# Window attention on the quarters of TensorE's array

## The chip, the cores and the metric

The kernel runs on one core of a Trainium2 chip. The metric is the device time of one execution in microseconds (us); lower is better. TensorE, VectorE (DVE), ScalarE (ACT), GpSimd (POOL) and the SP queue run their own instruction streams and meet through semaphores.

## The reference

Two layers in fp32 on x of shape (32, 56, 56, 48). Layer 0 makes a convolution per image from pooled features and adds it to x. Layer 1 is a shifted-window transformer block followed by a convolutional feed-forward part. The change lies in the attention part of layer 1, cut to what matters:

```python
h = roll(layer_norm(x) * g + b, (-3, -3))
xw = window_partition(h, 7)                 # 64 windows of 49 pixels per image
q, k, v = split_heads(xw @ w_qkv + b_qkv)   # 6 heads of 8
attn = softmax(q @ k.T * SCALE + rel_bias + mask)
o = (attn @ v) @ w_proj + b_proj
x = x + roll(window_reverse(o), (3, 3))
y = layer_norm(x)                           # goes to two convolutions with a GELU between
```

## The kernel before

Three stages run one after the other: `layer0`, `attention`, `feed_forward`. Layer 0 leaves its result in HBM as row chunks (`x1s`), attention writes x (`x2s`) and the second normalized y (`ys`), and the last stage reads both. Only `attention` is changed, with the constants and the packed weights that it uses.

Attention works on 128 chunks. A chunk is one row of 8 windows (7 pixel rows of 56) of two images; image 0 has its 48 channels on partitions 0 to 47, image 1 on 64 to 111. `each_chunk` calls `body` for the first two and last two chunks and in two loops of two chunks per turn between them. Each engine has its own `body`, an order written out by hand, in which work of four chunks is mixed: `body(n)` computes scores and softmax of chunk n, the normalization, queries, keys and value rows of n + 1, the output and projection of n - 1, and the second normalization of n - 2.

What one chunk does, before the change:

- `center` (L716): a matmul subtracts the channel mean. ScalarE copies the result (`xc`) and squares it twice, as fp32 and as a rounded part `sq_hi`; GpSimd makes `sq_lo`. `variance` sums both with two fp32r matmuls (L719, L720). ScalarE takes the logarithm and the exponential (L847, L851), VectorE multiplies to `h` (L1036), GpSimd copies `h` twice (L600).
- `queries`, `keys` (L716): one matmul each over both images. ScalarE writes the queries into a block-diagonal `qbd` in two parts (L859), GpSimd expands the keys to one masked copy per head, `kex`, one instruction per window (L614).
- `scores` (L674): per window one matmul with 98 weight columns (49 queries of two images) and 294 moving columns (49 keys of 6 heads). VectorE adds bias and mask per window (L1013), takes the maximum per duo of windows (L1025) and subtracts it (L1029); in the second duo GpSimd subtracts (L604). ScalarE takes the exponential (L882).
- `transposes` (L685): six per duo into the one buffer `ps_t`; ScalarE copies them to `pt` (L889), and the next duo's transposes wait for that copy (`pt_set`).
- `value_rows` (L745): per window one matmul; VectorE masks and copies (L1071). `values` (L700): per half chunk (4 windows) 24 matmuls for two heads at once, alternately on the left and right column half of the array. VectorE takes the reciprocal of the denominators and multiplies (L1045, L1049).
- `outputs` (L711) brings the result back to channels, ScalarE copies it (L874), `project` (L716) applies the projection, and VectorE adds the residual in two parts (L1061, L1063), rolled back by 3 pixels.
- `center2`, `variance2`, ScalarE and GpSimd: the second normalization, with the same split squares (L591); ScalarE applies the affine (L912).

An fp32 matmul is issued as two passes, each a weight load and a matmul; the trace counts passes. A transpose is one pass. SP issues eight DMAs per chunk: two loads of `xin`, two of `xres`, four stores. ScalarE copies the first 3 pixel columns behind the last (`wrap`, L832). PSUM has 8 banks in use: three for scores, two in `ps_t`, one for values and two in `ps_m` for all the rest.

Of the kernel before, what the change touches and what calls it, by code (L numbers as in the profile page):

```python
# [20 lines left out]
F32 = mybir.dt.float32  # L21
# [11 lines left out]
N = WS * WS  # L33
# [22 lines left out]
VW = 2 * HD + 2  # L56
HN = HEADS * N
DUOS = NWC // 2
# [5 lines left out]
class Pack:  # L64
# [27 lines left out]
    "wq": (PP, PP), "wk": (PP, PP), "wv": (PP, 2 * C), "wvd": (PP, PP), "wp": (PP, PP),  # L92
    "g1": (PP, 1), "be1": (PP, 1), "bq": (PP, 1), "bk": (PP, 1), "bv": (PP, 1), "bp": (PP, 1),
    "g2": (PP, 1), "be2": (PP, 1), "rel": (2 * N, HN), "masked": (2 * N, 4 * N),
    "center": (PP, PP), "sum": (PP, PP), "head": (PP, HEADS), "eps": (PP, 1),
    "couple": (2 * N, 2), "own": (2 * N, 2 * HD), "ident": (2 * N, 2 * N), "pick": (QP, 2 * N),
# [308 lines left out]
def attention(nc, x1s, pack, x2s, ys):  # L405
# [7 lines left out]
    with ctx:  # L413
# [3 lines left out]
        def sem(name):  # L417
# [3 lines left out]
        wqs, wks, wvs = sb("wqs", [PP, PP]), sb("wks", [PP, PP]), sb("wvs", [PP, 2 * C])  # L421
        bqs, bks, bvs, bps = sb("bqs", [PP, 1]), sb("bks", [PP, 1]), sb("bvs", [PP, 1]), sb("bps", [PP, 1])
        bias = sb("bias", [2 * N, 2, 2, HN])
        xin = [sb(f"xin{a}", [PP, WS, XP]) for a in range(2)]
        xres = [sb(f"xres{a}", [PP, WS, W]) for a in range(2)]
        xc = sb("xc", [PP, T2])
        sum_r = sb("sum_r", [PP, PP], F32R)
        sq = sb("sq", [PP, T2])
        sq_hi, sq_lo = sb("sq_hi", [PP, T2], F32R), sb("sq_lo", [PP, T2], F32R)
        sq2_hi, sq2_lo = sb("sq2_hi", [PP, T2], F32R), sb("sq2_lo", [PP, T2], F32R)  # L430
        lnv = sb("lnv", [PP, T2])
        rstd = sb("rstd", [PP, T2])
        h = sb("h", [PP, NWC, 2, N])
        ks = sb("ks", [PP, NWC, N])
        qbd = [sb(f"qbd{a}", [PP, NWC, 2 * N]) for a in range(2)]
        kex = [sb(f"kex{a}", [PP, NWC, HEADS, N]) for a in range(2)]
        vs = [sb(f"vs{a}", [2 * N, NWC * 2 * (HEADS // 2), VW]) for a in range(2)]
        s_sb = [sb(f"s{i}", [2 * N, 2, HN]) for i in range(2)]
        mx = [sb(f"mx{i}", [2 * N, 2, HEADS]) for i in range(2)]
        pt = [sb(f"pt{d}", [2 * N, 2, HEADS // 2, 2, N]) for d in range(DUOS)]  # L440
        rden = [sb(f"rden{half}", [QP, 4 * HEADS]) for half in range(2)]
        on = [sb(f"on{a}", [QP, NWC, C]) for a in range(2)]
        ot = sb("ot", [PP, WS, W])
        xo = [sb(f"xo{a}", [PP, WS, W]) for a in range(2)]
# [3 lines left out]
        ps_s = [ctx.enter_context(nc.psum_tensor(f"ps_s{i}", [128, 512], F32)) for i in range(3)]  # L448
        ps_t = ctx.enter_context(nc.psum_tensor("ps_t", [128, 2, 512], F32))
        ps_o = ctx.enter_context(nc.psum_tensor("ps_o", [128, 512], F32))  # L450


        ps_m = [ctx.enter_context(nc.psum_tensor(f"ps_m{i}", [128, 512], F32)) for i in range(2)]

        weights_in, xin_zeroed, zeroed, vones_set = sem("at_weights_in"), sem("xin_zeroed"), sem("at_zeroed"), sem("vones_set")
        o_rows_set = sem("o_rows_set")
        folded, bias_mm, biases, bp_mm, tables, pad_set = (
            sem("folded"), sem("bias_mm"), sem("biases"), sem("bp_mm"), sem("tables"), sem("pad_set"))
        sum_set = sem("sum_set")

        sq_split, sq2_split = sem("sq_split"), sem("sq2_split")
        x_in = [sem(f"at_x_in{a}") for a in range(2)]
        x2_out = [sem(f"x2_out{a}") for a in range(2)]
        y_out = [sem(f"y_out{a}") for a in range(2)]
        xres_in = [sem(f"xres_in{a}") for a in range(2)]
        wrapped = sem("wrapped")
        center_mm, xc_copied, squared, var_mm, ln_done, rstd_done, h_done, h_twice = (
            sem("center_mm"), sem("xc_copied"), sem("squared"), sem("var_mm"), sem("ln_done"), sem("rstd_done"), sem("h_done"),
            sem("h_twice"))
        q_mm, q_set, k_mm, k_set, v_mm, v_set, kex_set = (  # L470
            sem("q_mm"), sem("q_set"), sem("k_mm"), sem("k_set"), sem("v_mm"), sem("v_set"), sem("kex_set"))
        rden_set, o_set, ot_mm, ot_set, proj_mm, x2_set = (
            sem("rden_set"), sem("o_set"), sem("ot_mm"), sem("ot_set"), sem("proj_mm"), sem("x2_set"))
# [4 lines left out]
        s_mm, s_biased, max_done, shifted, pool_shifted, exp_done, t_mm, pt_set, pv_mm = (  # L478
            sem("s_mm"), sem("s_biased"), sem("max_done"), sem("shifted"), sem("pool_shifted"), sem("exp_done"), sem("t_mm"),
            sem("pt_set"), sem("pv_mm"))  # L480

        def w(name):
            return PACK2.at(cw, name)

# [23 lines left out]
        def by_head(tile):  # L508
            return tile[:, :, :].rearrange("q w (h k) -> q (w h) k", h=HEADS)

        def windows(ap):

            return ap.rearrange("c (r w k) -> c w r k", r=WS, w=NWC)

# [3 lines left out]
        def _(sp):  # L518
            sp.dma_start(cw[:, :], pack).then_inc(weights_in, 16)

            def load(n, a):
                for i in range(2):
                    sp.dma_start(xin[a][BO * i:BO * i + C, :, 0:W],
                                 x1s[n, C * i:C * i + C, :].rearrange("c (r n) -> c r n", r=WS)).then_inc(x_in[a], 16)

            def store(n, a):
                sp.wait_ge(x2_set, n + 1)
                sp.wait_ge(y_set, n + 1)
                for i in range(2):
                    sp.dma_start(x2s[n, C * i:C * i + C, :].rearrange("c (r n) -> c r n", r=WS),  # L530
                                 xo[a][BO * i:BO * i + C, :, :]).then_inc(x2_out[a], 16)
                    sp.dma_start(ys[n, C * i:C * i + C, :].rearrange("c (r n) -> c r n", r=WS),
                                 y[a][BO * i:BO * i + C, :, :]).then_inc(y_out[a], 16)

            def load_ahead(n, a):
                sp.wait_ge(center_mm, n + 1)
                load(n + 2, a)

            def load_residual(n, a):
                if at_edges(n)[0]:  # L540
                    sp.wait_ge(x2_set, n - 1)
                for i in range(2):
                    sp.dma_start(xres[a][BO * i:BO * i + C, :, :],
                                 x1s[n, C * i:C * i + C, :].rearrange("c (r n) -> c r n", r=WS)).then_inc(xres_in[a], 16)

            sp.wait_ge(xin_zeroed, 1)
            load(0, 0)
            load(1, 1)
            sp.wait_ge(zeroed, 1)
            for n in range(2):  # L550
                load_residual(n, n)
            for n in range(2):
                load_ahead(n, n)
            with sp.Fori(1, CHUNKS // 2 - 1) as m:
                for a in range(2):
                    load_ahead(m * 2 + a, a)
                    load_residual(m * 2 + a, a)
                    store(m * 2 + a - 2, a)
            for n in range(CHUNKS - 2, CHUNKS):
                load_residual(n, n % 2)  # L560
                store(n - 2, n % 2)
            for n in range(CHUNKS - 2, CHUNKS):
                store(n, n % 2)
# [5 lines left out]
        def _(pool):  # L569
# [3 lines left out]
            for a in range(2):  # L573
                pool.memset(qbd[a][:, :, :], 0.0)
                pool.memset(xres[a][:, :, :], 0.0)
                ins = pool.memset(y[a][:, :, :], 0.0)
            ins.then_inc(zeroed, 1)
            pool.wait_ge(weights_in, 16)
            for a in range(2):

                ins = pool.tensor_copy(vs[a][:, :, 2 * HD:VW],
                                       w("couple").unsqueeze(1).to_broadcast([2 * N, NWC * 2 * (HEADS // 2), 2]))
            ins.then_inc(vones_set, 1)

            def split_squares(n):
                pool.wait_ge(squared, n + 1)
                pool.tensor_tensor(sq_lo[:, :], sq[:, :], sq_hi[:, :], ALU.subtract).then_inc(sq_split, 1)

            def split_squares2(n):
                pool.wait_ge(squared2, n + 1)  # L590
                pool.tensor_tensor(sq2_lo[:, :], sq2[:, :], sq2_hi[:, :], ALU.subtract).then_inc(sq2_split, 1)  # L591

            def before_twice(n):

                pool.wait_ge(h_done, n + 1)
                if at_edges(n)[1]:
                    pool.wait_ge(v_mm, n * 2)

            def twice():
                pool.tensor_copy(h[:, :, 1, :], h[:, :, 0, :]).then_inc(h_twice, 1)  # L600

            def shift(n):
                pool.wait_ge(max_done, n * DUOS + 2)
                pool.tensor_tensor(by_head(s_sb[1]), by_head(s_sb[1]),  # L604
                                   mx[1][:, :, :].rearrange("q w h -> q (w h)").unsqueeze(2).to_broadcast([2 * N, 2 * HEADS, N]),
                                   ALU.subtract).then_inc(pool_shifted, 1)

            def keys(n, a):

                pool.wait_ge(k_set, n + 1)  # L610
                if at_edges(n)[0]:
                    pool.wait_ge(s_mm, n * NWC - NWC)
                for win in range(NWC):
# [981 lines left out]
```

## Time and profile before

| | us |
|---|---|
| median of 3 runs | 3709.49 (3706.65 to 3709.59) |
| the profiled execution's own time | 3707.4 |
| its span, first to last instruction | 3705.6 |
| PE busy | 3445.4 (93%) |
| DVE busy | 2853.4 (77%) |
| ACT busy | 2389.6 (64%) |
| POOL busy | 2047.7 (55%) |
| mean granted TensorE clock | 0.972 of full speed |

Busy time is the time in which at least one instruction of the engine runs; matmuls are pipelined, so their records overlap, and the distance from one start to the next says more than a record's length. The clock is 1.00 where the array runs at 2.4 GHz and 0.50 at 1.2 GHz. The profiled execution took 1.8 us more than its span.

### The profile page before, as it was taken

How to read it: one execution, taken by the hardware profiler on the slowest of the kernel's cores; microseconds unless marked ns; L12 is line 12 of the kernel's file. 1: busy time of each engine (PE TensorE's matmuls, PEld its weight loads, DVE VectorE, ACT ScalarE, POOL GpSimd, SP SyncE). 2: the span in 40 equal slices, each digit the busy share in tenths (PEclk: the TensorE clock that was granted, in tenths of full speed). 3: DMA queues.
4: the chain of work that ended last, by engine and by line, in shares of the span. 5: the costliest groups of instructions: out<-in, count | busy, mean ns of one | idle time of the engine just before them, and what ended most of it. 6: DMA issues, size and time to landing. Idle time of an engine off the chain costs nothing. (4 is left out here: it accounts for less than half of the span.)

```text
span 3705.6 us, 94419 instructions
## 1 busy us (share of the span) xinstructions
PE 3445.4 (93%) x31796; PEld 2390.5 (65%) x31796; DVE 2853.4 (77%) x4885; ACT 2389.6 (64%) x4324; POOL 2047.7 (55%) x2188
## 2 busy tenths in 40 slices
PE   6898879999999999999999999999599999999998
PEld 3566557667667667667667667666366666666665
DVE  4543457777777777777777777777599999999998
ACT  3432337777777777777777777777366666666665
POOL 1110146666666666666666666666255555555554
PEclk8898789999999999999999999999799999999999
DMA  4331021111111111111111111111566665666663
GB/s 113 105 103 44 22 61 40 38 35 39 38 34 39 38 35 39 38 34 39 38 34 39 38 34 39 38 34 37 82 109 113 109 108 99 105 105 112 111 104 62
DMA packets 235789, 230.18 MB, mean 62 GB/s; under 512 B 118064, under 2 KB 230704, under 8 KB 232624
## 3 DMA queue, kind: packets, MB, share of 16 engines
q1 hardware_dynamic: 235696, 229.14, 30.6%
q8 instruction: 35, 0.57, 0.1%
q14 instruction: 58, 0.48, 0.1%
HBM read 151.26 MB, written 77.76 MB: 62 GB/s over the span
## 5 line engine op out<-in xcount | busy, mean ns | idle before, releaser
L614 POOL TENSOR_TENSOR kex<-ks,cw 112x294 f32<-112x294 f32 x1024 | 734.2, 750 | 232.8 <-ACT ks L866 232.8
L674 PE MATMUL ps_s<-kex,qbd 112*98 112x294 f32 x2048 | 592.4, 411 | 0.0
L1256 POOL TENSOR_TENSOR ya_lo<-ya,ya_hi 128x464 fp32r<-128x464 f32 x224 | 284.4, 1270 | 310.1 <-DVE ya_hi L1426 210.4
L1013 DVE TENSOR_TENSOR s<-ps_s,bias 98x294 f32<-98x294 f32 x1024 | 434.9, 454 | 14.1 <-PE ps_s L674 2.2
L674 PEld LDWEIGHTS ps_s<-kex,qbd 112*98 112x98 f32 x2048 | 318.4, 165 | 165.3 <-issue 80.2
L889 ACT ACTIVATE pt<-ps_t 98x588 f32<-98x588 f32 x512 | 338.1, 660 | 120.2 <-PE ps_t L685 114.5
L1025 DVE TENSOR_REDUCE mx<-s 98x12 f32<-98x588 f32 x512 | 390.8, 763 | 13.2
L1262 POOL TENSOR_TENSOR hid_a_lo<-hid_a,hid_a_hi 128x448 fp32r<-128x448 f32 x224 | 298.1, 1331 | 183.9 <-ACT hid_a_hi L1353 183.9
L1029 DVE TENSOR_TENSOR s<-s,mx 98x588 f32<-98x588 f32 x384 | 388.5, 1012 | 13.1
L685 PEld LDWEIGHTS ps_t<-cw,s 98*98 98x98 f32 x3072 | 300.6, 127 | 101.8 <-issue 46.9
L882 ACT ACTIVATE s<-s 98x588 f32<-98x588 f32 x512 | 354.4, 692 | 4.5 <-DVE s L1029 1.4
L685 PE MATMUL ps_t<-cw,s 98*98 98x98 f32 x3072 | 348.1, 248 | 1.3 <-ACT lnv L902 1.3
L1429 DVE TENSOR_TENSOR yb_sp<-yb,yb_sp 48x464 fp32r<-48x464 f32 x224 | 340.2, 1519 | 7.8
L700 PEld LDWEIGHTS ps_o<-vs,pt 98*49 98x49 f32 x12288 | 303.1, 126 | 65.9 <-issue 53.2
L700 PE MATMUL ps_o<-vs,pt 98*49 98x18 f32 x12288 | 328.4, 199 | 0.0
L1299 PE MATMUL ps_b<-ya,cw 128*64 128x448 f32 x1344 | 279.2, 550 | 31.7 <-DMA yb<-y_chunks 31.7
L745 PEld LDWEIGHTS ps_m<-wvs,h 112*98 112x98 f32 x2048 | 197.5, 167 | 108.3 <-issue 100.6
L1313 PE MATMUL ps_a<-ya_hi,wa_hi 128*128 128x448 f32 x672 | 261.7, 389 | 0.0
L1360 ACT ACTIVATE hid_b<-ps_b,cw 128x448 f32<-128x448 f32 x112 | 81.2, 725 | 277.3 <-PE ps_b L1301 277.3
L745 PE MATMUL ps_m<-wvs,h 112*98 112x96 f32 x2048 | 238.4, 260 | 18.5 <-POOL h L600 12.2
L1313 PE MATMUL ps_a<-ya_hi,wa_lo 128*128 128x448 f32 x672 | 249.9, 372 | 0.0
L1313 PE MATMUL ps_a<-ya_lo,wa_hi 128*128 128x448 f32 x672 | 249.8, 372 | 0.0
(164 smaller groups left out, 7186.2 us busy)
## 6 DMA issues: line engine op xcount, KB each, us to landing
ya<-y_chunks SPq DMA_DIRECT2D x64, 532.9 KB, 6.4
y_chunks<-y SPq DMA_DIRECT2D x256, 76.1 KB, 1.8
xin<-x_chunks SPq DMA_DIRECT2D x256, 73.5 KB, 2.5
xres<-x_chunks SPq DMA_DIRECT2D x256, 73.5 KB, 1.9
x_chunks<-xo SPq DMA_DIRECT2D x256, 73.5 KB, 1.8
out<-xr SPq DMA_DIRECT2D x32, 588.0 KB, 5.4
yb<-y_chunks SPq DMA_DIRECT2D x96, 177.6 KB, 8.1
xr<-x_chunks SPq DMA_DIRECT2D x32, 514.5 KB, 5.7
```

The lines of the kernel that those rows point to most:

```text
L614: pool.tensor_tensor(kex[a][:, win, :, :], ks[:, win, :].unsqueeze(1).to_broadcast([PP, HEADS, N]), w("head").unsqueeze(2).to_broadcast([P ...
L674: pe.matmul(ps_s[win % 3][0:2 * N, 0:HN], qbd[a][:, win, :], kex[a][:, win, :, :].rearrange("c h k -> c (h k)"), start=True, stop=True).th ...
L685: mm = pe.transpose(ps_t[0:2 * N, i, part], s_sb[d % 2][:, i, part], w("ident"))
L700: mm = pe.matmul(ps_o[BO * img:BO * img + N, (i * (HEADS // 2) + j) * VW:(i * (HEADS // 2) + j + 1) * VW], pt[win // 2][:, win % 2, j, img ...
L745: mm = pe.matmul(ps_m[1 - half][0:2 * N, i * 2 * C:(i + 1) * 2 * C], h[:, win, :, :].rearrange("c i k -> c (i k)"), wvs[:, :], start=True, ...
L882: act.activation(s_sb[d % 2][:, :, :], s_sb[d % 2][:, :, :], ACT.Exp).then_inc(exp_done, 1)
L889: act.activation(pt[d][:, :, :, :, :].rearrange("q w j i n -> q w (j i n)"), ps_t[0:2 * N, :, 0:HN], ACT.Copy).then_inc(pt_set, 1)
L1013: dve.tensor_tensor(s_sb[i][:, k, :], ps_s[win % 3][0:2 * N, 0:HN], bias[:, low, int(win == NWC - 1), :], ALU.add).then_inc(s_biased, 1)
L1025: dve.tensor_reduce(mxi, s4, AX.X, ALU.max).then_inc(max_done, 1)
L1029: dve.tensor_tensor(s4, s4, mxi.unsqueeze(2).to_broadcast([2 * N, 2 * HEADS, N]), ALU.subtract).then_inc(shifted, 1)
L1313: pe.matmul(bank[:, 0:T1], weights[:, kw, :], pixels(image[:, :], c, kw), start=kw == 0 and i == 0, stop=False)
L1429: dve.tensor_tensor(yb_sp[BO:PP, px], yb[a][0:C, px], yb_sp[0:C, px], ALU.subtract).then_inc(y_b_set, 1)
```

## The change

Everything in attention's inner part is laid out anew, for tiles of the array:

- Queries and keys are laid out in four row groups, each 24 channels on 32 partitions: (image, heads 0 to 2) and (image, heads 3 to 5). Scores are matmuls with 24 contracted rows, 49 weight columns and 147 moving columns, and two windows write to the two column halves. They fill four PSUM banks, one per row group; all four windows of a half chunk are done before VectorE starts.
- `center`, `queries_and_keys`, `value_rows`, `values`, `outputs` and `project` use the 64x64 quarters: contraction over one image's or one window's partitions, output on one partition half. Values are one head per matmul, 48 weights x 9 columns per half chunk instead of 24 x 18.
- VectorE adds, takes maxima and subtracts over a half chunk (113 x 1176) in one instruction; it subtracts in the first half chunk, GpSimd in the second. ScalarE takes one exponential per half chunk. Transposes are of 113 columns.
- The split of squares goes: GpSimd squares in fp32 (`squares`, `squares2`), and `variance` is one plain fp32 matmul. GpSimd also takes the second affine from ScalarE. The copy `h` twice goes; `kex` has three copies per head group, made in two instructions. The wrap columns of `xin` and `xres` are loaded by DMA, so SP issues 12 DMAs per chunk. The residual is two parts and a copy of 3 columns.
- PSUM: four banks `ps_s`, two `ps_t`, two `ps_m`. `ps_s` also takes queries, keys, value rows and center; `ps_m` takes variances, values, outputs and the projection; `ps_t` takes center2. So several groups wait for the reader of the group before. `tiled()` is a wait on a semaphore that is set long before, ahead of groups in tiles.

```diff
+            def tiled():
+                pe.wait_ge(weights_in, 16)
...
             def transposes(n, d):
-                t = n * DUOS + d
-                pe.wait_ge(exp_done, t + 1)
-                if not isinstance(n, int) or t >= 1:
-                    pe.wait_ge(pt_set, t)
-                for i in range(2):
-                    for j in range(HEADS // 2):
-                        part = slice(j * 2 * N, (j + 1) * 2 * N)
-                        mm = pe.transpose(ps_t[0:2 * N, i, part], s_sb[d % 2][:, i, part], w("ident"))
+                half, p = d // 2, d % 2
+                for j in range(TR):
+                    for img in range(2):
+                        mm = pe.transpose(ps_t[0:QP, img, j * 2 * BO:j * 2 * BO + QP],
+                                          s_sb[half][:, p * TR + j, 2 * img:2 * img + 2, :].rearrange("q g k -> q (g k)")[:, 0:QP],
+                                          w("ident"))
                 mm.then_inc(t_mm, 1)
...
+            def scores(n, half, a):
+                tiled()
+                pe.wait_ge(kex_set, n * 2 + half + 1)
+                for p in range(2):
+                    for u in range(2):
+                        win = half * NH + p * 2 + u
+                        for g in range(4):
+                            group = slice(32 * g, 32 * g + C // 2)
+                            mm = pe.matmul(ps_s[rows(u, N), g, p * TR * N:(p + 1) * TR * N], q[a][group, win, :],
+                                           kex[a][group, win, :, :].rearrange("c j k -> c (j k)"), start=True, stop=True)
+                mm.then_inc(s_mm, 1)
...
+                        for j in range(TR):
+                            for g in range(2):
+                                for img in range(2):
+                                    to = ((p * 2 + u) * TR + j) * VW
+                                    block = (img * NH + p * 2 + u) * TR + j
+                                    mm = pe.matmul(ps_m[rows(img, N), g, to:to + VW], pt[half * 2 + p][rows(g, N), img, j, u, :],
+                                                   vs[a][rows(g, N), half, block, :], start=True, stop=True)
                 mm.then_inc(pv_mm, 1)
...
+            def shift(n):
+                dve.wait_ge(max_done, n * 2 + 1)
+                part = s_sb[0][:, :, :, 0:N]
+                dve.tensor_tensor(part, part, mx[0][:, :, :].unsqueeze(3).to_broadcast([QP, 2 * TR, 4, N]),
+                                  ALU.subtract).then_inc(shifted_a, 1)
...
             def shift(n):
-                pool.wait_ge(max_done, n * DUOS + 2)
+                pool.wait_ge(max_done, n * 2 + 2)
+                part = s_sb[1][:, :, :, 0:N]
+                pool.tensor_tensor(part, part, mx[1][:, :, :].unsqueeze(3).to_broadcast([QP, 2 * TR, 4, N]),
+                                   ALU.subtract).then_inc(shifted_b, 1)
```

TensorE's new order in `body(n)`, waits in brackets:

```python
# scores(n,0); [o_set of n-1, half 0] variance(n+1), variance2(n-2)
# [xc2_copied, pt_set, exp_done] transposes(n-1,2); [pt_set] transposes(n-1,3)
# [s_biased, h_done] queries_and_keys(n+1); [ln_done, ln2_done, pt_set] values(n-1,1)
# [q_set, k_set, x_in] scores(n,1); [o_set] outputs(n-1); [exp_done] transposes(n,0)
# [ot_set] project(n-1); [s_biased] value_rows(n+1); center(n+2)
# [pt_set] transposes(n,1); [pt_set, x2_set] center2(n-1); values(n,0)
```

The other engines' orders in `body(n)`:

```python
# VectorE: outputs(n-1,0), add(n,0), maxima(n,0), normalize(n+1), shift(n),
#          outputs(n-1,1), add(n,1), residual(n-1), value_rows(n+1), maxima(n,1)
# ScalarE: centered2(n-2), exps(n-1,1), ln, rsqrt(n+1), transposed(n-1,2), ln2(n-2), transposed(n-1,3),
#          rsqrt2(n-2), queries, keys(n+1), exps(n,0), outputs(n-1), transposed(n,0), centered(n+2), transposed(n,1)
# GpSimd:  squares2(n-2), keys(n+1), normalize2(n-2) with the affine, squares(n+2), shift(n)
```

## Rows read from the trace of the kernel before

**Rows 1.** Busy time (instructions) by engine, clock and DMA in one chunk.

```profile
1499.68:1515.97 16.29, 15.46 (x198) 11.33 (x198) 12.93 (x25) 12.33 (x25) 10.89 (x13) 1.00 0.16 37
```

**Rows 2.** TensorE in order of time: start us, length us, line, shapes, count, idle before.

```profile
1502.96 0.93 PE L745 MATMUL ps_m<-wvs,h 112*98 112x96 f32 x8 [0.20 <-POOL h L600]
1503.82 1.28 PE L700 MATMUL ps_o<-vs,pt 98*49 98x18 f32 x48
1504.94 0.91 PE L711 MATMUL ps_m<-cw,on 113*48 113x49 f32 x32
1505.77 0.93 PE L745 MATMUL ps_m<-wvs,h 112*98 112x96 f32 x8
1506.54 0.68 PE L685 MATMUL ps_t<-cw,s 98*98 98x98 f32 x6
1507.06 0.83 PE L716 MATMUL ps_m<-ot,cw 112*112 112x392 f32 x2
1507.73 1.16 PE L674 MATMUL ps_s<-kex,qbd 112*98 112x294 f32 x4
1508.72 0.82 PE L716 MATMUL ps_m<-xin,cw 112*112 112x392 f32 x2
...
1510.57 1.16 PE L674 MATMUL ps_s<-kex,qbd 112*98 112x294 f32 x4
1511.65 1.28 PE L700 MATMUL ps_o<-vs,pt 98*49 98x18 f32 x48
...
1516.07 0.90 PE L716 MATMUL ps_m<-h,wqs 112*112 112x392 f32 x2 [0.72 <-ACT lnv L902]
```

**Rows 3.** TensorE in two short stretches, passes on two column halves.

```profile
1503.82 0.23 PE L700 MATMUL ps_o<-vs,pt 98*49 98x18 f32 x2
...
3003.98 2.48 PE L1299 MATMUL ps_b<-ya,cw 128*64 128x448 f32 x12
```

**Rows 4.** Groups of the other engines, 1000 to 2500 us, and two single subtractions.

```profile
L614 POOL TENSOR_TENSOR kex<-ks,cw 112x294 f32<-112x294 f32 x735 | 526.9, 750 | 161.5 <-ACT ks L866 161.5
...
L1013 DVE TENSOR_TENSOR s<-ps_s,bias 98x294 f32<-98x294 f32 x736 | 312.5, 454 | 8.8
L1025 DVE TENSOR_REDUCE mx<-s 98x12 f32<-98x588 f32 x367 | 280.1, 763 | 9.5
...
L882 ACT ACTIVATE s<-s 98x588 f32<-98x588 f32 x368 | 254.7, 692 | 2.2
...
L604 POOL TENSOR_TENSOR s<-s,mx 98x588 f32<-98x588 f32 x92 | 107.9, 1172 | 0.0
...
L622 POOL TENSOR_TENSOR y<-xc,rstd 112x392 f32<-112x392 f32 x92 | 93.3, 1015 | 151.1 <-ACT rstd L908 151.1
...
L1049 DVE TENSOR_TENSOR on<-ps_o,rden 113x192 f32<-113x192 f32 x184 | 65.8, 358 | 6.3
...
L1045 DVE RECIPROCAL rden<-ps_o 113x24 f32<-113x24 f32 x183 | 55.4, 303 | 0.0
...
1501.12 1.32 DVE L1029 TENSOR_TENSOR s<-s,mx 98x588 f32<-98x588 f32 x1
...
1510.44 0.77 DVE L1029 TENSOR_TENSOR s<-s,mx 98x588 f32<-98x588 f32 x1
```

**Rows 5.** ScalarE in order of time, behind TensorE and ahead of it.

```profile
1507.26 0.66 ACT L889 ACTIVATE pt<-ps_t 98x588 f32<-98x588 f32 x1 [0.83 <-PE ps_t L685]
...
1515.38 0.59 ACT L902 ACTIVATE lnv<-ps_m,cw 112x392 f32<-112x392 f32 x1 [0.19 <-PE ps_m L720]
```

**Rows 6.** The end of attention in two stretches, columns as in rows 1.

```profile
2597.00:2604.00 7.00, 4.22 (x63) 2.78 (x60) 2.50 (x6) 3.59 (x7) 1.01 (x1) 1.00 0.16 46
2604.00:2611.00 7.00, 5.49 (x84) 3.79 (x83) 0.67 (x2) 2.23 (x4) 1.01 (x1) 0.55 0.02 5
```

**Rows 7.** DMA queues and a load's landing, 700 to 2300 us.

```profile
q1 hardware_dynamic: 106624, 59.58, 15.1%
...
xin<-x_chunks SPq DMA_DIRECT2D x196, 73.5 KB, 2.5
```

More of the change, by code:

```diff
@@ L654, in _ @@
             pe.wait_ge(weights_in, 16)
-            for i, name in enumerate(("wq", "wk", "wvd")):
-                mm = pe.matmul(ps_m[0][0:PP, i:i + 1], w(name), w("be1"), start=True, stop=True)
+            pe.wait_ge(banks_zeroed, 1)
+            for i, (name, count) in enumerate((("wq", QM), ("wk", QM), ("wvp", C))):
+                for c in range(2):
+                    mm = pe.matmul(ps_t[rows(c, count), 0, i:i + 1], w(name)[0:C, :], w("be1")[0:C, :], start=True, stop=True)
             mm.then_inc(bias_mm, 1)
@@ new lines, in center, with variance @@
+            def center(n, a):
+                for img in range(2):
+                    for half in range(2):
+                        px = xin[a][rows(img, C), :, SHIFT + half * HW2:SHIFT + half * HW2 + HW2]
+                        mm = pe.matmul(ps_s[rows(half, BO), 2 + img, 0:HP], w("center")[rows(img, C), rows(img, BO)],
+                                       px.rearrange("c r (w k) -> c w r k", w=NH), start=True, stop=True)
+                mm.then_inc(center_mm, 1)
+            def variance(n):
+                pe.wait_ge(squared, n + 1)
+                pe.matmul(ps_m[0:PP, 0, 0:T2], w("sum"), sq[:, :, :], start=True, stop=True).then_inc(var_mm, 1)
@@ new lines, in queries_and_keys @@
+            def queries_and_keys(n):
+                pe.wait_ge(h_done, n + 1)
+                for bank, weights, signal in ((0, wqs, q_mm), (2, wks, k_mm)):
+                    for half in range(2):
+                        for img in range(2):
+                            mm = pe.matmul(ps_s[rows(img, QM), bank + half, 0:HP], weights[rows(half, C), :],
+                                           h[rows(half, C), img, :, :], start=True, stop=True)
+                    mm.then_inc(signal, 1)
@@ new lines, in value_rows @@
+            def value_rows(n):
+                for img in range(2):
+                    for win in range(NH):
+                        for half in range(2):
+                            for g in range(2):
+                                to = (img * NH + win) * (C // 2)
+                                mm = pe.matmul(ps_s[rows(g, N), half, to:to + C // 2], h[rows(half, C), img, win, :],
+                                               wvs[rows(half, C), g * (C // 2):(g + 1) * (C // 2)], start=True, stop=True)
+                mm.then_inc(v_mm, 1)
@@ L710, in outputs @@
+                mm.then_inc(pv_mm, 1)
+            def outputs(n):
+                for win in range(NH):
                     for img in range(2):
-                        mm = pe.matmul(ps_m[1][BO * img:BO * img + C, win * N:(win + 1) * N], on[a][:, win, :],
-                                       w("pick")[:, img * N:(img + 1) * N], start=True, stop=True)
+                        for half in range(2):
+                            mm = pe.matmul(ps_m[rows(half, C), img, win * N:(win + 1) * N], on[rows(img, N), half * NH + win, :],
+                                           w("ident")[rows(img, N), rows(img, N)], start=True, stop=True)
@@ L749, in project @@
             def project(n):
+                tiled()
                 pe.wait_ge(ot_set, n + 1)
-                misc(1, w("wp"), ot[:, :, :], proj_mm)
+                for half in range(2):
+                    for img in range(2):
+                        mm = pe.matmul(ps_m[rows(img, C), half, 0:HP], w("wp")[rows(half, C), :],
+                                       ot[rows(half, C), img, :].rearrange("c (w r k) -> c r w k", w=NH, r=WS), start=True, stop=True)
+                mm.then_inc(proj_mm, 1)
@@ L772, in body @@
+                if after2:
+                    pe.wait_ge(x_in[a], m * 64 + 128)
                 scores(n, 1, a)
                 if before:
[L774 to L776 removed]
+                    tiled()
+                    pe.wait_ge(o_set, n * 2)
+                    outputs(n - 1)
+                pe.wait_ge(exp_done, n * 2 + 1)
                 transposes(n, 0)
[L779 to L782 removed]
```

695 lines of the change are left out of this document (317 added, 378 removed).

## The prediction

> **What bounds the kernel now.** First the table of stretches: over most of the span attention repeats itself, one chunk every 16.3 us (one L604 subtraction per chunk, 92 in 1500 us [rows 4]). In one chunk of 16.29 us TensorE is busy 15.46 us at the full clock, VectorE 12.93, ScalarE 12.33, GpSimd 10.89 [rows 1]. Next one chunk on TensorE in order of time [rows 2]: its groups stand end to start, and the one gap is 0.72 us before the queries, waiting for ScalarE's logarithm. So TensorE's stream sets the chunk. Start to start the groups cost (passes are instructions; an fp32 matmul is two): scores 4 passes of 294 columns 0.99 us, four times 3.96; values 48 passes 1.12, twice 2.24; six transposes 0.52, four times 2.08; value rows 8 passes 0.86, twice 1.72; the outputs' 32 passes 0.83; a 392-column fp32 matmul 0.67, five times 3.35. Sum 14.18; the other 2.11 are two split variances, the gap and the changes of tiling.
>
> **What a pass costs when the array is split.** The values matmuls already use two column halves: the first two start in one instant, and 48 passes take 1.12 us, 46.7 ns for each two [rows 2, 3]. In the last stage 12 passes of 448 columns on two halves take 2.48 us with their tail [rows 3], where a 392-column pass on the whole array takes 0.335 [rows 2] and 12 of 448 would take 4.6. So halves run beside each other. The trace holds nothing on four quarters or on eight tiles of 32x64. Bounds: four passes in one step (46.7 ns with 49 weight columns, where the time seems to be the weight load, since 98 weight columns take 86 to 108 ns, or 0.168 us with 196 moving columns), or no better than two at once (23.3 ns a pass). I take the first, as nothing in the two-half rows shows a common limit; both ends are kept.
>
> Skill against trace: the Trainium skill (TensorE: Matmul & The Clock Gate, "Wait — 56ns, not 53.3ns?") says that matmul starts are never closer than about 25 ns however small the matmul is. The values passes start 23.3 ns apart on the mean and two of them at once [rows 3], so it does not hold across tiles as stated. By it the path below would grow by 288 passes x 13.3 ns to 18.7 us, an estimate of 4015 us in all. The mechanism is the first rival below, priced from rows.
>
> **TensorE's groups after the change** (passes per chunk, array time): scores 2 x 32 passes of 147 columns, eight tiles, 4 steps x 0.124 = 0.50 each (two at once: 1.98); values 2 x 96 passes of 49 weights, 24 steps x 46.7 ns = 1.12 each (two at once 2.24); value rows 64 passes, 0.75 (1.49); outputs 32 passes, 0.41 (0.83); queries and keys 16 passes, 0.67 (1.34); center and project 0.34 each (0.67); center2 0.67; two variances now in plain fp32, 0.67 each; transposes 24, of 113 columns for 98, 0.60 per six. Sum 10.2 us, where nearly 16 were. So the array stops being the bound, and the waits between engines take over; passes grow from 198 to 414 per chunk.
>
> **The other engines.** VectorE: an add of 294 columns takes 454 ns and a maximum of 588 763 ns, so a column takes 1.05 ns and the start 0.145 us [rows 4]. Add of 1176 columns 1.38, twice; maximum 1.38, twice; subtraction of the first half 1.37 to 2.4 (588 columns take 0.77 to 1.33) [rows 4], taken 1.45; normalize 0.56; value rows one copy 0.55 for two products; outputs 2 x 0.70; residual, two parts of 196 columns (0.35 each) and a 3-column copy behind a wait, 1.0. Sum 10.5, where 12.93 was. ScalarE: four Square passes, the affine, the wrap and one query pass go; exponentials 2 x 1.2 (twice 692 ns less one start) for 4; sum about 9. GpSimd: keys 2 x 588 columns (each 1.17 as in the 588-column subtraction, or 1.50, twice the 294-column product) 2.7; two squares and one product of 392, 1.0 each; the affine 0.5 to 1.1, taken 0.85; subtraction of 1176 columns 2.2 (2.34 is twice 588); sum 8.9 for 10.89. SP issues 12 loads and stores for 8; the added four bring 3 columns each, land in about 2.5 us as the long ones do [rows 7] and are needed a chunk later: nothing. More DVE and GpSimd memsets at the start lie beside the weights' load: nothing, within 3 us.
>
> **The path of one chunk.** With one ps_t and one ps_m for everything, TensorE must stop between dependent groups. The pieces: six transposes until the next may overwrite ps_t: weight load 0.09, record 0.76 (0.68 scaled), 0.04 to ScalarE, copy 0.66, 0.07 back, 1.62 us [rows 2, 5]. Values until their outputs are on SBUF: tail 0.16 (1.28 less 1.12), 0.1 to VectorE (as from ScalarE to TensorE here), reciprocal and product 0.70 [rows 4], 0.07 back: 1.05 with rounding up. A change of tiling costs 0.09 (1510.57 + 0.99 to 1511.65 [rows 2]). From o_set on:
> - variance, variance2: 1.34
> - transposes 2, then 3 behind the copy; values behind the second copy: 2 x 1.62 = 3.24 (queries and keys hide in the second)
> - values half 1: 1.22 with the switch; until its outputs: 1.05 (scores half 1 hide in it)
> - outputs 0.41, tail 0.2, ot copy 0.57, back 0.07 (transposes 0 hide in it): 1.25
> - project, value rows, center: 1.43
> - transposes 1 and the copy, with a switch: 1.72; center2 and switches 0.77
> - values half 0: 1.22; until its outputs: 1.05 (scores half 0 of the next chunk hide in it).
> Sum 14.29. Some six places have stacked waits on TensorE's queue at about 0.1 each, and the loop's branch once in two chunks: 14.9.
> A second ring is nearly as long: transposes 2 and copy 1.62, transposes 3, queries and keys 1.47, tail 0.34, ScalarE's queue (copy, rsqrt2, queries, keys) 1.4, then GpSimd keys 2.7, product 1.0, affine 0.95, squares 1.0, subtraction 2.2, ScalarE's exp 1.2, three hand-overs 0.2: 14.1 (13.3 to 15.0 by the bounds). So GpSimd's order has under 1 us to spare.
> The forecast: 128 chunks x (16.29 - 14.9) = 178 us off. The profiled execution took 3707.4 us (span 3705.6), so 3529; the median shown is 2 us above it: **3530 us**. Its own range is 14.2 to 15.6 us per chunk, 3440 to 3620.
>
> **Rivals.**
> - Passes are issued no faster than now, or the row halves do not overlap (slower side). Place: values, value rows, outputs. At 23.3 ns a pass the path gains 2 x 1.12 + 0.75 + 0.41 = 3.4 us, 18.3 per chunk, 3707 + 128 x 2.0 = 3965 us. It decides from 16.5 ns a pass on (1.39 us over the path's 288 passes beyond 11.7). For it: no row shows more than two at once. Against it: the two starts in one instant. Chance 0.12.
> - The clock. In the attention's tail TensorE was busy 4.22 of 7 us at clock 1.00, and the next 7 us ran at 0.55, largely the 1.2 GHz level [rows 6]. After the change its array works some 10.2 of 14.9 us with gaps up to 0.9 us. If the clock fell for good, the path's 8 us of streams double: near 23 us, 4570 us. Against it: gaps are short and even. Chance 0.06.
> - GpSimd's ring is the bound: keys 1.5 each, affine 1.1, subtraction 2.34 and VectorE in the way, 15.6 to 16 us: 3620 to 3670 us. Chance 0.14.
> - Waits overlap better: the path has 0.9 us stalls but VectorE, ScalarE shorter than I add; 13.6 to 14.2 us, 3360 to 3440. Chance 0.12.
> - The code of TensorE's loop (two chunks, 828 passes, each a weight load and a matmul, 1656 instructions besides waits) is twice as long. Now no instruction fetch runs in the loop [rows 7]. If each turn fetched, a landing of 2.5 us [rows 7] for 64 turns: +160, 3690 us. Chance 0.04. The Trainium skill (Runtime: NRT & Kernel Launch, "Instruction fetch mechanics") gives TensorE room for 2048 instructions; that the present loop never fetches agrees.
> - The forecast: 0.52.
>
> **How the numbers follow.** Faster by over 0.2% (what a measurement here can tell): forecast, GpSimd ring, better overlap and most of the code case, 0.79; within 0.2%: 0.03; slower 0.18. The 8-in-10 range leaves out the upper part of the slow cases and a little below: 3390 to 3790.
>
> **What would show it.** Right: values groups of 96 passes in about 1.2 us; TensorE idle some 4 us a chunk, waiting for ScalarE's pt copies (twice 0.9) and VectorE's outputs; clock 1.00; VectorE near 70%. Wrong: values at 2.2 us; clock 0.5 in attention; exp of half 1 waited for by transposes 2 (GpSimd); instruction packets in the loop. I would be plainly wrong if the period were under 13.5 or over 16 us.

## The result, and the profile after

| | before | after |
|---|---|---|
| median, us | 3709.54 (3706.65 to 3711.96, 4 runs) | 4868.32 (4841.17 to 4906.22, 4 runs) |
| the profiled execution's own time | 3707.4 | 4875.6 |
| its span | 3705.6 | 4873.8 |
| PE / DVE / ACT / POOL busy | 93 / 77 / 64 / 55% | 84 / 51 / 41 / 34% |
| mean granted TensorE clock | 0.972 | 0.682 |

The ratio is 1.313 (1.304 to 1.322): slower by 31%, where 5% faster was forecast. Every engine has a smaller share of busy time than before; in microseconds only TensorE's rose (4093.4 for 3445.4), though its array work was forecast to fall. Two lines of the page say where to look. First the granted clock in 40 slices, then the queues:

```profile
PEclk8988555555555556555565555555555899999999
...
q1 hardware_dynamic: 563376, 231.04, 26.7%
q8 instruction: 588, 9.63, 0.8%
```

From the fifth slice to the thirty-first, which is attention, the clock is at half for most of the time. And the instruction queue brought 588 packets of 16 KB, where the kernel before had 35 over the whole run and none in its loop [rows 7]. In 1600 us inside the loop there are 279, 9 for each turn of two chunks. Next the stretches, as in [rows 1]: 500 us, then one whole turn, its quiet chunk, and the 11 us around the branch:

```profile
1000.00:1500.00 500.00, 397.65 (x8017) 287.21 (x8014) 193.25 (x269) 179.56 (x288) 151.85 (x137) 0.56 0.16 27
...
1990.08:2041.37 51.29, 39.53 (x844) 28.01 (x843) 20.13 (x28) 18.72 (x31) 15.73 (x15) 0.60 0.16 28
2001.25:2022.93 21.68, 19.68 (x415) 14.15 (x414) 10.04 (x15) 9.30 (x15) 7.81 (x7) 0.58 0.13 19
1990.08:2001.25 11.17, 4.21 (x79) 2.50 (x75) 1.89 (x3) 0.46 (x1) 0.36 (x1) 0.50 0.25 44
```

A turn takes 51.3 us, 25.6 per chunk for 16.29 [rows 1]. Between one variance and the next a chunk takes 21.7 us, largely at the low clock (0.58 on the mean); around the branch TensorE is busy 4.2 of 11.2 us. TensorE in order of time through that place, and what it waited for on "issue" between 1000 and 2500 us (us in total, times, longest), show what it does there:

```profile
1989.78 1.16 PE L711 MATMUL ps_m<-vs,pt 49*49 49x9 f32 x48
1995.24 0.76 PE L689 MATMUL ps_s<-kex,q 24*49 24x147 f32 x12 [4.30 <-issue]
1998.66 1.22 PE L689 MATMUL ps_s<-kex,q 24*49 24x147 f32 x20 [2.67 <-issue]
1999.81 1.65 PE L660 MATMUL ps_m<-sq,cw 112*112 112x392 f32 x2
...
2004.73 0.85 PE L698 MATMUL ps_t<-cw,s 113*113 113x113 f32 x6 [0.83 <-ACT pt L891]
2005.51 0.56 PE L667 MATMUL ps_s<-h,wqs 48*56 48x196 f32 x8
2005.88 0.51 PE L667 MATMUL ps_s<-h,wks 48*56 48x196 f32 x8
2006.42 1.28 PE L711 MATMUL ps_m<-vs,pt 49*49 49x9 f32 x96
...
2018.19 2.19 PE L711 MATMUL ps_m<-vs,pt 49*49 49x9 f32 x96
2020.31 1.26 PE L689 MATMUL ps_s<-kex,q 24*49 24x147 f32 x32
...
2031.53 0.40 PE L719 MATMUL ps_m<-cw,on 49*48 49x49 f32 x3 [1.13 <-issue]
...
PE ps_s L689 <- issue: 185.4, 59, 4.4
PE ps_m L719 <- issue: 23.3, 22, 1.5
```

The releaser "issue" means that nothing the profile knows was awaited. The three such gaps, 4.30, 2.67 and 1.13 us, are 8.1 us in this turn; on the mean of the 29 turns it is 7.1 (208.7 us). The first lies at the branch; the second cuts a group of scores after 12 passes, the third a group of outputs ahead of its last 3, where nothing new is waited for, and that rules out another engine for these two. The same rows show the clock: one and the same group of 96 values passes takes 1.28 us at one place and 2.19 at another. Groups of the other engines, 1000 to 3500 us, which answer to [rows 4], kept their forecast durations. VectorE's add waits for TensorE, and GpSimd's keys wait for ScalarE's copy of what TensorE computes (behind the bar: busy us, one instruction in ns, idle us before it):

```profile
L999 DVE TENSOR_TENSOR s<-ps_s,bias 113x1176 f32<-113x1176 f32 x195 | 269.9, 1384 | 431.4 <-PE ps_s L689 431.2
L1006 DVE TENSOR_REDUCE mx<-s 113x24 f32<-113x1176 f32 x195 | 267.6, 1372 | 3.4
...
L884 ACT ACTIVATE s<-s 113x1176 f32<-113x1176 f32 x196 | 235.8, 1203 | 3.7 <-POOL s L584 3.7
L594 POOL TENSOR_TENSOR kex<-ks,cw 120x588 f32<-120x588 f32 x196 | 228.3, 1187 | 1291.6 <-ACT ks L875 1291.6
L584 POOL TENSOR_TENSOR s<-s,mx 113x1176 f32<-113x1176 f32 x98 | 214.2, 2186 | 2.2 <-DVE mx L1006 2.2
```

So there are two suspects, both of them rivals of the prediction with small chances: the code of TensorE's loop and its clock.

### The profile page after: what moved, and what is told of

It reads as the page before. It is cut to its first block and busy times, and to the rows that moved or that the text cites. A ratio compares the mean times of both kernels' runs of the same rounds, so it can differ in the third digit from the quotient of the medians.

```text
span 4873.8 us, 145311 instructions
## 1 busy us (share of the span) xinstructions
PE 4093.4 (84%) x59452; PEld 2838.9 (58%) x59452; DVE 2506.7 (51%) x3610; ACT 2001.1 (41%) x3172; POOL 1653.9 (34%) x1420
## 5 line engine op out<-in xcount | busy, mean ns | idle before, releaser
L594 POOL TENSOR_TENSOR kex<-ks,cw 120x588 f32<-120x588 f32 x256 | 298.2, 1187 | 1659.4 <-ACT ks L875 1659.4
L698 PEld LDWEIGHTS ps_t<-cw,s 113*113 113x113 f32 x3072 | 591.5, 283 | 298.6 <-issue 155.3
L698 PE MATMUL ps_t<-cw,s 113*113 113x113 f32 x3072 | 679.6, 386 | 101.8 <-ACT pt L891 101.1
L689 PE MATMUL ps_s<-kex,q 24*49 24x147 f32 x8192 | 340.2, 424 | 381.6 <-issue 371.0
L999 DVE TENSOR_TENSOR s<-ps_s,bias 113x1176 f32<-113x1176 f32 x256 | 354.3, 1384 | 543.3 <-PE ps_s L689 542.9
L711 PEld LDWEIGHTS ps_m<-vs,pt 49*49 49x49 f32 x24576 | 498.0, 180 | 178.9 <-issue 164.6
L891 ACT ACTIVATE pt<-ps_t 113x588 f32<-113x588 f32 x512 | 338.6, 661 | 487.9 <-PE ps_t L698 487.6
L711 PE MATMUL ps_m<-vs,pt 49*49 49x9 f32 x24576 | 505.2, 220 | 3.9 <-ACT pt L891 2.5
L1006 DVE TENSOR_REDUCE mx<-s 113x24 f32<-113x1176 f32 x256 | 351.4, 1373 | 4.5
L884 ACT ACTIVATE s<-s 113x1176 f32<-113x1176 f32 x256 | 307.9, 1203 | 5.5 <-POOL s L584 5.5
```

The lines of the kernel that those rows point to most:

```text
L594: pool.tensor_tensor(kex[a][:, wins, :, :], ks[:, wins, :].unsqueeze(2).to_broadcast([QR, NH, TR, N]), w("head").unsqueeze(1).unsqueeze(3) ...
L689: mm = pe.matmul(ps_s[rows(u, N), g, p * TR * N:(p + 1) * TR * N], q[a][group, win, :], kex[a][group, win, :, :].rearrange("c j k -> c (j ...
L698: mm = pe.transpose(ps_t[0:QP, img, j * 2 * BO:j * 2 * BO + QP], s_sb[half][:, p * TR + j, 2 * img:2 * img + 2, :].rearrange("q g k -> q ( ...
L711: mm = pe.matmul(ps_m[rows(img, N), g, to:to + VW], pt[half * 2 + p][rows(g, N), img, j, u, :], vs[a][rows(g, N), half, block, :], start=T ...
L884: act.activation(part, part, ACT.Exp).then_inc(exp_done, 1)
L891: act.activation(pt[d][:, :, :, :, :].rearrange("q i j u k -> q i (j u) k"), ps_t[0:QP, :, 0:2 * TR * BO].rearrange("q i (b k) -> q i b k" ...
```

## The experiments

Times are medians; the kernel before, run beside them, took 3706.8 to 3708.7.

### The code of the loop: e1 to e4, e7

A turn of TensorE's loop is 1701 instructions in the trace of after and 846 in that of before. The instruction packets have 16,384 bytes. The Trainium skill (Runtime: NRT & Kernel Launch, "Instruction fetch mechanics") counts 256 instructions to such a block, and by that 1701 are 6.6 blocks. Whether they lie in 7 or in 8 blocks depends on where the loop begins. e1 changes only that, for TensorE alone (the diffs here are shortened):

```diff
-                with body.engine.Fori(start, end) as m:
+                # for TensorE alone; first instruction at slot 0 of a block
+                with nc.Fori(start, end, engines=..., head_slot={e: 0}) as m:
```

> The changed kernel with one thing different: the first instruction of each of TensorE's attention loops is placed at the start of a 16 KB block of code. A turn has 1701 instructions of 64 B, 6.64 blocks: it spans 7 blocks from a block's start, and 8 from most other places. Theory (the code no longer stays resident, because 8 blocks and the one behind them are wanted): no 16 KB packets of the instruction queue in the loop (now 9 per turn of two chunks), the 4.2 and 3.0 us stalls at the head of the turn gone. If these stalls are also what holds TensorE's clock down: 14 to 16 us per chunk, 3450 to 3700 us. If the clock falls by itself, because the array is only some two thirds busy: only the 8 us per turn go, 21.7 us per chunk, about 4350 us with the clock still near 0.56. Rival (the count of instructions decides, not the placement): nothing changes, 4870 us.

Measured: 3916.7 us (3910.6 to 3956.4), ratio to before 1.060 (1.054 to 1.066). No instruction packet in 700 to 2300 us. The same instructions in the same order, moved by under one block, take 952 us less. Both theories of the expectation are half right: the fetches are gone, and the clock rose (0.56 to 0.80 in 1000 to 2000 us) but not to 1.00. Two chunks of it, wholly at the one clock and wholly at the other:

```profile
1523.53:1538.07 14.54, 12.46 (x415) 9.10 (x415) 9.06 (x14) 9.42 (x16) 7.81 (x7) 1.00 0.16 22
1634.78:1657.86 23.08, 21.58 (x414) 16.00 (x414) 10.02 (x14) 9.38 (x15) 7.81 (x8) 0.50 0.16 27
```

At 1.00 a chunk takes 14.54 us, at 0.50 it takes 23.08 us. TensorE in the fast one has three idle places a chunk, 0.83 and 0.75 us for the pt copies, as the path foretold, and 0.39 for the keys:

```profile
1523.53 0.85 PE L704 MATMUL ps_t<-cw,s 113*113 113x113 f32 x6 [0.83 <-ACT pt L898]
1524.31 0.56 PE L673 MATMUL ps_s<-h,wqs 48*56 48x196 f32 x8
1524.68 0.51 PE L673 MATMUL ps_s<-h,wks 48*56 48x196 f32 x8
1525.22 1.28 PE L717 MATMUL ps_m<-vs,pt 49*49 49x9 f32 x96
1526.89 0.75 PE L695 MATMUL ps_s<-kex,q 24*49 24x147 f32 x32 [0.39 <-ACT ks L882]
1527.57 0.58 PE L725 MATMUL ps_m<-cw,on 49*48 49x49 f32 x32
...
1532.11 0.91 PE L740 MATMUL ps_t<-xo,cw 112*112 112x392 f32 x2 [0.75 <-ACT pt L898]
1532.95 1.28 PE L717 MATMUL ps_m<-vs,pt 49*49 49x9 f32 x96
1534.26 0.75 PE L695 MATMUL ps_s<-kex,q 24*49 24x147 f32 x32
...
1538.07 0.85 PE L704 MATMUL ps_t<-cw,s 113*113 113x113 f32 x6 [0.75 <-ACT pt L898]
```

e2 leaves the placement as it was and announces the branch back at the top of each turn:

```diff
-                with body.engine.Fori(start, end) as m:
+                with nc.Fori(start, end, engines=..., hint_back_edge=True) as m:
```

> The changed kernel with a hint instruction at the top of each turn of TensorE's attention loops that announces the branch back. Theory (code refetched each turn): the same 9 blocks are fetched, but the 4.2 us stall at the branch shrinks to under 0.5 us; the 3.0 us stall 24 passes later may stay. 4870 - 64 x 4.2 = 4600 us if the clock stays, less if it rises. Rival (the gap at the turn isn't a fetch at the branch): no change.

Measured: 4062.4 us (4027.1 to 4082.3), ratio 1.093 (1.086 to 1.100), and no fetch in the loop at all, which neither side had expected. Either the one added instruction shifted the loop into 7 blocks, or the hint keeps the code in place. e7 tells these apart, with the hint and `head_slot={e: 140}`:

> The changed kernel with the hint of e2, but its loop placed at slot 140 of a 16 KB block, so that it surely spans 8 blocks (140 + 1702 slots = 7.2 blocks). Theory A (e2 lost its fetches because the hint stops the fetch of a ninth block, which pushed the first one out): no instruction packets in the loop, about 4000 us. Theory B (e2 lost them because the added instruction moved the loop so that it spans 7 blocks; the hint itself only brings the first block early): 9 packets per turn remain, the stall at the branch is short, the clock stays low, 4500 to 4700 us.

Measured: 4038.3 us (4016.4 to 4045.8), 49 instruction packets in the whole run and none in 700 to 2300 us. Theory A stands in that with the hint 8 blocks stay. That without it they do not rests on e3 below, and on the changed kernel itself, whose starting place is not on record: that it lies in 8 blocks is inferred from its 9 packets per turn. That the block fetched behind the loop's end pushes out its first is my reading; it fits 9 packets per turn for 8 blocks, but no record names the block, and no run tested it. Why e7 and e2 are 122 and 146 us behind e1, without fetches either (e7's clock is at 0.70 to 0.76 where e1's is at 0.78 to 0.81), stays open.

Does it need the new tiling at all? e3 and e4 are the kernel before, with four instead of two chunks in a turn of TensorE's loop (1690 instructions), which begins at slot 200 or at slot 0 of a block; what an odd number of turns leaves over stands behind the loop:

```diff
-                with body.engine.Fori(start, end) as m:
-                    body(m * 2, m, 0, low)
-                    body(m * 2 + 1, m, 1, low)
+                with nc.Fori(0, count, engines=..., head_slot={e: 200}) as mm:
+                    for k in range(2):
+                        m = mm * 2 + (start + k)
+                        body(m * 2, m, 0, low)
+                        body(m * 2 + 1, m, 1, low)
```

> The kernel before, with the same work, but TensorE's attention loop holds four chunks a turn (about 1690 instructions, as long as the changed kernel's) and begins at slot 200 of a 16 KB block, so that it spans 8 blocks. Theory (refetching is a matter of code alone): about 9 instruction packets per turn of four chunks and stalls of about 7 us at the head of each of 31 turns, some 220 us more: 3900 to 3950 us if the clock stays at 1.00; if stalls alone bring the clock down, over 4300 us. Rival (the stalls belong to the new quarter tiling): 3710 us and no instruction packets in the loop.

> As the last one, but the loop begins at slot 0 of a block and spans 7 blocks. Theory (7 blocks and the one behind them stay resident, 8 do not): no instruction packets in the loop, 3710 us within 5. Rival (1690 instructions are too many wherever they lie): as the last one, 3900 us or more.

Measured: e3 3830.0 us (3814.7 to 3860.1), ratio 1.032 (1.029 to 1.035), with 203 instruction packets in 1600 us, 9 per turn again; e4 3708.3, ratio 1.0003 (0.9994 to 1.0013), none. The fetches are a matter of length and place, not of tiling. Their price was over-estimated: 122 us over 30 turns is 4.1 us per turn, not 7, and the clock's drops are in it. TensorE of e3 at a branch:

```profile
609.93 0.83 PE L729 MATMUL ps_m<-ot,cw 112*112 112x392 f32 x2
613.38 1.23 PE L687 MATMUL ps_s<-kex,qbd 112*98 112x294 f32 x4 [2.62 <-POOL kex L627]
614.45 1.28 PE L729 MATMUL ps_m<-xin,cw 112*112 112x392 f32 x2
```

The gap carries GpSimd's name here, probably since a semaphore was set during it; in the kernel before, the same place has no gap [rows 2]. The clock drops behind the gap (the next 392-column matmul takes 1.28 us, not 0.83) but comes back: its mean is 0.954 over the run for 0.972. The section of the Trainium skill named above gives TensorE 128 KiB, refilled in blocks of 16 KiB, prefetched in sequence, with a stall at a branch whose target isn't in the current window of two blocks. The packets' size agrees, and so does a stall at a branch; the window of two blocks does not, since e4 branches back over 7 blocks without a packet. That what counts is the blocks touched, 7 of them without a packet and 8 only with the branch announced, is what e1, e3, e4 and e7 add.

### The clock: e5, e6, e8, e9, e10

What remains in e1 is a clock of 0.80. e5 fills the idle places with matmuls of no use:

```diff
+            def filler(bank, count):
+                for _ in range(count):
+                    pe.matmul(bank[0:QP, 392:512], w("ident"), w("rel")[:, 0:120], start=True, stop=True)
...
                     transposes(n - 1, 2)
+                    pe.wait_ge(ln_done, n + 2)
+                    filler(ps_m[:, 0, :], 3)
                     pe.wait_ge(pt_set, n * DUOS - 1)
...
+                    pe.wait_ge(xc_copied, n + 3)
+                    filler(ps_s[:, 3, :], 3)
                     pe.wait_ge(pt_set, n * DUOS + 2)
                     center2(n - 1, 1 - a)
```

> The changed kernel with the loop at the start of a block (as e1) and work for TensorE in its two longest idle places per chunk: three matmuls of 113x113 weights and 120 columns, results unused, ahead of the wait for the pt copy before transposes 3, and three ahead of the same wait before center2 (e1 had TensorE idle 0.75 to 0.83 us there, and its clock at 1.00 for 59% of the attention). A 120-column pass is about 0.1 us, so three matmuls (six passes) take 0.6 us of a gap of 0.8 and delay nothing at the full clock. Theory (the idle places at the full clock bring the clock down; filled, it stays up): clock 0.95 to 1.00, one chunk in the 14.5 us that e1 shows at the full clock, 3707 - 128 x 1.8 = 3480 us. Rival (the clock falls because passes on quarters and 24-row tiles leave most of the array unused, however busy the engine looks): the clock stays near 0.8, 3900 us or more.

Measured: 3662.1 us (3658.7 to 3668.6), ratio 0.9875 (0.9858 to 0.9891). Adding work took 255 us away. The clock is at 0.91, neither the 0.95 of the theory nor the 0.8 of the rival. e6 adds `filler(ps_t[:, 0, :], 2)` ahead of the wait for the keys:

> As the last one, with two more such matmuls (0.4 us) ahead of the wait for the keys, before the scores of half 1 (idle 0.39 us in e1). Theory: clock at least as high as in the last one; if that one is at 1.00 already, the same time within 10 us. If three and three do not hold the clock and this does, the rest of the idle time decides: 3480 us here and 3600 to 3900 there.

Measured: 3610.7 us (3604.6 to 3614.1), ratio 0.974 (0.972 to 0.976): faster than before by 2.6%. One chunk of it at the full clock, then 500 us of it:

```profile
1508.00:1522.67 14.67, 14.22 (x431) 10.84 (x431) 9.95 (x14) 9.41 (x16) 7.82 (x7) 1.00 0.21 34
...
1000.00:1500.00 500.00, 479.70 (x13947) 361.66 (x13937) 322.76 (x454) 304.04 (x485) 254.77 (x229) 0.96 0.25 40
```

Is it that TensorE is occupied, or how much of the array it uses? e8 is e6 with a small corner of the weights in each added matmul (three of them also write to another bank than in e6):

```diff
-                    pe.matmul(bank[0:QP, 392:512], w("ident"), w("rel")[:, 0:120], start=True, stop=True)
+                    pe.matmul(bank[0:N, 392:512], w("ident")[64:88, 0:N], w("rel")[64:88, 0:120], start=True, stop=True)
```

> As e6 (three, three and two matmuls in the idle places, time 3611 us there), but each added matmul uses only a 24x49 corner of the weights instead of 113x113; columns and passes are the same, so TensorE is occupied for the same time. Theory A (what holds the clock up is that TensorE is occupied): as e6, 3600 to 3620 us, clock 0.94. Theory B (what counts is how much of the array works): the clock stays as in e1, about 0.8, 3850 to 3920 us.

Measured: 3896.9 us over four runs (3827.9 to 3927.9); the ratio, 1.040 (1.032 to 1.047), is that of the two fastest, whose mean is 3854.4. So small matmuls win 20 to 62 us over e1's 3916.7, at most a fifth of the 306 that the large ones win. Its 500 us, then one chunk of it at the full clock:

```profile
1000.00:1500.00 500.00, 490.28 (x12469) 361.70 (x12467) 292.76 (x406) 271.51 (x435) 226.06 (x203) 0.82 0.22 36
...
1506.01:1520.85 14.84, 14.21 (x431) 10.61 (x431) 10.03 (x14) 9.42 (x16) 7.81 (x7) 1.00 0.23 37
```

TensorE is busy 98% of the time here and 96% in e6, with the same passes and columns, and the clock is 0.82 for 0.96. A low clock raises the busy share by itself, so compare at 1.00: 14.21 of 14.84 us here (a chunk with the branch in it, 0.50 us idle), 14.22 of 14.67 in e6. So for the clock the busy share is the wrong view: work on a small part of the array does not do what work on the whole does. Which of the fewer rows, the fewer columns and the shorter weight load makes the difference was not tested. The quarters and the 24-row tiles of this change are also small parts. That they are what lowers its clock is inferred from e8 and the kernel before: that one is busy 15.46 of 16.29 us [rows 1], no more than e8, and is at 1.00.

The rest of the idle time, e9 (one more filler ahead of the variance) and e10 (four, three, three and two, with the hint because of the length):

> As e6, with one more 113x113 matmul of 120 columns (0.2 us) ahead of the wait for VectorE's outputs before the variance, where e6 had TensorE idle 0.24 us. Theory (remaining idle time decides): fewer drops of the clock, 3580 to 3605 us. Rival (the 0.55 us at the branch alone sets the rest): 3611 us.

> More filling than there is idle time: four, three, three and two such matmuls, and the hint of e2, since the turn is now longer than 7 blocks of code. Each one beyond the gaps costs its 0.2 us on the path: three of them, 0.6 us per chunk, 77 us. Theory: clock 1.00 throughout, chunk 14.7 + 0.5 us: about 3570 us. If it is slower than e9, the filling costs more than the last drops of the clock do.

Measured: e9 3610.5 us (3606.2 to 3611.3), no gain over e6, as its rival had it (3611); e10 3620.7 (3619.5 to 3626.9), ratio 0.977 (0.976 to 0.978), at a clock of 1.00 in 1500 to 2000 us and 15.4 us per chunk. Filling pays until the gaps are full; behind that the last drops are as cheap as what keeps them away. The times of both theories were too low, by at least 5 and by 50 us.

### Which engine subtracts: e11, e12

From e6, the subtraction of the second half moved to VectorE (e11) or that of the first half to GpSimd, ahead of the keys (e12):

```diff
                 maxima(n, 1)
+                shift(n, 1)        # e11, VectorE; shift(n) goes from GpSimd's body
...
                     squares2(n - 2)
+                shift(n, 0)        # e12, GpSimd; shift(n) goes from VectorE's body
                 if after:
                     keys(n + 1, 1 - a)
```

> As e6 (3611 us), with the maxima of the second half chunk subtracted on VectorE as well (1.38 us there, 2.19 us on GpSimd). In e6 VectorE is busy 10 of 15.4 us per chunk, GpSimd 7.9, and the exponentials of half 1 wait 1.1 us for GpSimd's subtraction. Theory (TensorE's groups and the copies between them set the chunk, nothing on VectorE or GpSimd does): 3590 to 3630 us. Rival (GpSimd's ring, forecast at 14.1 us, is the bound): the exponentials come 0.8 us earlier, 128 x 0.8 = 100 us less, about 3510 us. Other rival (the outputs of half 0 now stand behind the subtraction on VectorE's queue, 1.4 us later): 3700 us or more.

> As e6 (3611 us), with both subtractions on GpSimd (2.19 us each), that of half 0 ahead of the keys in its queue. GpSimd is then busy 10.1 us a chunk. It waits 5.65 us for the keys' activation at the place where the subtraction goes in. Theory (GpSimd has room there): the subtraction runs in its idle time, and the exponentials of half 0 come no later than now, since VectorE's normalize stood ahead of it: 3590 to 3640 us. Rival (GpSimd's ring has under 1 us to spare, as forecast): the keys come late, 1.2 to 2.2 us per chunk, 3770 to 3890 us.

Measured: e11 3602.5 us (3593.9 to 3611.1), ratio 0.971 (0.969 to 0.973); e12 3604.8 us (3594.7 to 3610.9), ratio 0.971 (0.970 to 0.973). With e6's 3610.7 that is one time, within 0.3%. 1.4 us more on VectorE's queue, and 2.2 us more on GpSimd's, change nothing where they were put. GpSimd in e12, at that place:

```profile
1530.45 2.45 POOL L590 TENSOR_TENSOR s<-s,mx 113x1176 f32<-113x1176 f32 x1 [2.53 <-DVE mx L1025]
1533.58 2.33 POOL L600 TENSOR_TENSOR kex<-ks,cw 120x588 f32<-120x588 f32 x2 [0.68 <-ACT ks L894]
```

The added subtraction runs in time in which GpSimd would be idle, and the keys behind it still wait for ScalarE.

## Why the prediction was wrong

- **The path of one chunk held.** Forecast 14.9 us, measured 14.54 at the full clock in e1; by the prediction's own arithmetic that is 3707 - 128 x 1.75 = 3483 us, against 3530 forecast. That it came so close is in part luck, for two errors in it cancel, as the next point shows.
- **Four quarters at once: right.** The record of 96 values passes is 1.28 us long, as that of 48 was before [rows 2]. The first rival (no faster passes) is out. The array's groups sum to 12.5 us, not 10.2 (start to start in e1's fast chunk: scores 0.68 for 0.50, queries and keys 0.91 for 0.67, six transposes 0.78 for 0.60). The idle time was shorter to match: 14.54 less 12.46, 2.1 us, where "some 4" was foretold.
- **The other engines: right.** Add 1.38, maximum 1.37, subtraction 1.38 and 2.19, exponential 1.20, all as foretold; keys 1.19 each, at the lower bound. GpSimd's ring (0.14) was not the bound: e11 takes 0.8 us out of it, and that is worth 8 us at most. That it "has under 1 us to spare" fits the trace. In e1's fast chunk ScalarE ends the exponentials of half 1 at 1536.08, and the transposes that need them start at 1536.56, behind the variances:

```profile
1534.86 1.22 ACT L891 ACTIVATE s<-s 113x1176 f32<-113x1176 f32 x1 [1.31 <-POOL s L590]
...
1536.56 0.76 PE L704 MATMUL ps_t<-cw,s 113*113 113x113 f32 x6
```

e12's 2.2 us lie ahead of the keys, outside this stretch of the ring, so it does not measure what the ring could bear.

- **The code (0.04): the first step that failed.** The count was there (1656 instructions besides waits, twice as long), but it was compared with a room of 2048 instructions instead of asking in how many blocks they lie, and priced as one landing of 2.5 us, 160 us in all. Measured: three stalls, 7.1 us per turn on the mean, some 440 us over 62 turns. Placement alone is worth 952 us, since without the stalls the clock also rises (0.56 to 0.80).
- **The clock (0.06): the second.** "Gaps are short and even" was taken as a reason against it, and the array's use was read from occupied time. Without any fetch the clock was still 0.80 (e1), and it came back with 1.6 us of useless full-array matmuls per chunk (e6), not with useless small ones (e8). The price given, near 23 us per chunk, was right: 23.08 us measured wholly at the low clock (e1). What failed is the reason to think it would not happen.
- **The two were weighed as separate accidents.** They are one chain: more and smaller passes make the code longer and leave more of the array unused, the stalls lower the clock further (0.56 with them, 0.80 without), and at the low clock TensorE's groups are slower. In the turn shown, 25.6 us per chunk is 21.6, largely at the low clock, and half of 8.1. The Trainium skill (TensorE: Matmul & The Clock Gate, "A second HAM failure mode: psum-queue depth-cycling") describes a kernel whose brief idling between groups of matmuls makes its clock oscillate between the two levels. e1's trace agrees in that its clock goes to and fro between them, with gaps of 0.4 to 0.8 us; but e8 has these gaps filled and its clock is hardly higher, so idling is not the whole cause here. The chance of 0.06 left both out.

From after to a kernel that beats before: placement 952 us, filling 306, and 98 below before (e6). What is left to the 3483 us of a chunk at 14.54 us is the pause at each branch, the filling's surplus and the last drops of the clock (0.96); no run takes them apart.

## What to carry to other kernels

When a change multiplies TensorE's instructions, count the 16 KB blocks that a turn's code touches (here 7 ran from what was there, 8 did not) and look for instruction packets inside the loop; if there are any, place the loop's head or announce its branch before judging the change. When it splits the array into tiles, read the granted clock beside the busy share, and price the array's time at both levels. If a stage loses the clock with waits in it, a few full-size matmuls of no use, in gaps that are there anyway, are a cheap test, and may be the cure.

## What was not expected of the hardware

- 1690 instructions in 7 blocks ran without a fetch (e4, 3708 us), the same in 8 blocks fetched 9 packets per turn (e3, 3830 us), and 8 blocks with an announced branch fetched none (e7).
- More work made the kernel 8% faster: 3917 to 3611 us by eight matmuls of 113x113 weights and 120 columns per chunk (e1, e6). The same with 24x49 weights gave 3897 (e8).
